# Embedding: rounded turns from one multiplication into 32-bit integers, in place of adding and subtracting a large constant

## The chip, the cores and the metric

The kernel runs on one core of a Trainium2 chip. The metric is the device time of one execution in microseconds (us); lower is better. The program is a small vision model: a sine and cosine embedding of four images, one attention layer with relative positions, an MLP, a second attention layer and a mixture of experts. The change touches only the embedding, the first some 295 us of the span.

## What the embedding must compute

For every coordinate and each of six frequencies (powers of two), the reference takes sin and cos of 2 pi times coordinate times frequency, and multiplies the 6912 features of a token with a weight matrix:

```python
xb = 2.0 * jnp.pi * xyz[..., None] * freq_bands
feat = jnp.concatenate([jnp.sin(xb), jnp.cos(xb)], axis=-1)
feat = feat.reshape(b, n, -1)
return jnp.einsum('bnf,of->bno', feat, W)
```

The kernel reduces the angle first: the turn is x f minus the nearest whole number, which lies within half a turn, and sin and cos are taken of 2 pi times that.

## The kernel before

`embed_phase` works through four images. The 576 coordinates of an image lie in five chunks of up to 128 partitions, x[128, 5, 512] (512 tokens along the free side). A **group** is one frequency for two chunks (1024 elements for each partition), twelve in an image (pair groups), or, for the last chunk, whose 64 coordinates are there twice, two frequencies at once (512 elements), three in an image. So an image has 15 groups, and the buffers `near`, `turn`, `feat` and `parts` are rings of three groups (`NF`). The order of each engine is written out by hand; semaphores count groups.

For each group, by engine and line:

- VectorE (DVE): `shift` (L202) writes x f + 12582912 into `near`; adding that constant (1.5 times 2 to the 23) leaves no room for a fraction in a float32. `whole` (L207) subtracts it again in place, so `near` is x f rounded to a whole number. `reduce` (L215) makes turn = x f - near in one instruction with two tensor operands. `absolute` (L221) writes the turn without its sign bit over `near`. For pair groups, `rest` (L232) subtracts from the features their first part.
- ScalarE (ACT): the sine of `turn` (L357), the cosine as a sine of a quarter turn minus the absolute turn (L359), and for pair groups `first_parts` (L370), a rounded copy of half the features.
- TensorE (PE): for the first chunk of a group `native`, 16 float32 matmuls (L427); for the second chunk `split`, 16 matmuls on the parts (L443 in the first group, else L445, and L447). All add into four PSUM banks. `split` waits for `rest` of its group.

In the first image alone the weights are split too: ACT rounds them (L364, queued behind the group's cosine), DVE subtracts (`split_weights`, L226), and PE's `split` waits for that. The first image also carries the class row: its statistics ahead of group 4 on DVE (L295, L297), square roots ahead of group 6 on ACT, its normalization ahead of group 8 on DVE (L301, L304).

In `image` (L307 to L330) DVE runs ahead in this order: `whole(g + 1)`, `reduce(g)`, `shift(g + 2)`, `absolute(g)`, `rest(g - 1)`, and in the first image `split_weights(g)`; before the loop stand two `shift` and one `whole` (L333 to L335). `shift(g + 2)` waits for the cosine of group g - 1, which reads the same third of the ring. At group 1 of each later image `take_sums` copies the sums of the image before out of PSUM (L238, L241), and the first matmul of the new image waits for it. Images 2 and 3 run in a loop, the fourth is written out. Numbers in this document count images from the first to the fourth and groups from 0 to 14.

Of the kernel before, what the change touches and what calls it, by code (L numbers as in the profile page):

```python
# [8 lines left out]
ALU = mybir.AluOpType  # L9
ACT = mybir.ActivationFunctionType  # L10
AX = mybir.AxisListType
F32 = mybir.dt.float32
F32R = mybir.dt.float32r
BF16 = mybir.dt.bfloat16
U32 = mybir.dt.uint32


B = 4
N = 512
# [25 lines left out]
EXPERTS, TOPK, HID = 8, 2, 4 * D  # L45
HC = HID // 128

MAGIC = 12582912.0
NO_SIGN = 0x7FFFFFFF
TWO_PI = 6.283185307179586  # L50
EPS = 1e-5
# [1 line left out]
GROUPS = [(c0, 2, f) for c0 in (0, 2) for f in range(BANDS)] + [(4, 1, j) for j in range(BANDS // 2)]  # L53
UNITS = [(c0 + i, f) for c0, n, f in GROUPS for i in range(n)]
NE = len(GROUPS)
# [8 lines left out]
def stand_alone(eng, passed):  # L64


    eng.sem_inc(passed, 1)


def embed_phase(nc, s):  # L70

    NF = 3
    sem = s.sem
# [1 line left out]
    raw_in = [sem(f"raw_in{g}") for g in range(NE)]  # L75
    freq_in, ident_in, cls_in, zeroed = sem("freq_in"), sem("ident_in"), sem("cls_in"), sem("zeroed")
    consts_set, edges_set = sem("consts_set"), sem("edges_set")
    shifted, rounded, turn_done, aturn_done = sem("shifted"), sem("rounded"), sem("turn_done"), sem("aturn_done")
    sin_done, cos_done, feat_free, passed = sem("sin_done"), sem("cos_done"), sem("feat_free"), sem("turns_passed")
    w_hi, w_lo, hi_done, lo_done = sem("w_hi"), sem("w_lo"), sem("hi_done"), sem("feat_lo")  # L80
    pairs = [g for g in range(NE) if GROUPS[g][1] == 2]
# [10 lines left out]
    with ExitStack() as ctx:  # L92
        sb = lambda n, sh, dt=F32: ctx.enter_context(nc.sbuf_tensor(n, sh, dt))
        x = sb("x", [128, 5, N])
# [2 lines left out]
        feat = sb("feat", [128, NF, 2, 2, N])  # L97
        w_parts = sb("w_parts", [128, NPAIR, 2, 2, D], F32R)
        parts = sb("parts", [128, NF, 2, 2, N], F32R)
        near = sb("near", [128, NF, 2, N])  # L100
        turn = sb("turn", [128, NF, 2, N])
        aturn = near
        tokens, h1_tok = sb("tokens", [128, 4, D]), sb("h1_tok", [128, 4, D])
        b2_rows, base = sb("b2_rows", [128, D]), sb("base", [128, 4, D])
        stats, mean_var = sb("stats", [128, 4, 6]), sb("mean_var", [128, 4, 2])
# [2 lines left out]
        freq = sb("freq", [128, NU])  # L108
# [78 lines left out]
        def _(dve):  # L187
# [1 line left out]
            dve.memset(eps[:, 0:1], EPS).then_inc(consts_set, 1)  # L189
            dve.memset(eps[:, 1:2], EPS * EPS).then_inc(consts_set, 1)  # L190

            def shift(b, g, first):
                c0, n, f = GROUPS[g]
                u, r = first_unit[g], g % NF
                if f == 0:
                    for c in range(c0, c0 + n):
                        dve.wait_ge(x_in[c], b * 16 + 16)
                if g >= NF or not first:
                    dve.wait_ge(cos_done, b * NE + g - NF + 1)
                if not first:  # L200
                    stand_alone(dve, passed)
                dve.tensor_scalar(near[:, r, 0:n, :], x[:, c0:c0 + n, :], freq[:, u:u + 1], MAGIC, ALU.mult, ALU.add).then_inc(shifted, 1)  # L202

            def whole(b, g):
                n, r = GROUPS[g][1], g % NF
                dve.wait_ge(shifted, b * NE + g + 1)
                dve.tensor_scalar(near[:, r, 0:n, :], near[:, r, 0:n, :], MAGIC, None, ALU.subtract).then_inc(rounded, 1)  # L207

            def reduce(b, g, first):
                c0, n, f = GROUPS[g]  # L210
                u, r = first_unit[g], g % NF
                dve.wait_ge(rounded, b * NE + g + 1)
                if g >= NF or not first:
                    dve.wait_ge(sin_done, b * NE + g - NF + 1)
                dve.scalar_tensor_tensor(out=turn[:, r, 0:n, :], in0=x[:, c0:c0 + n, :], scalar=freq[:, u:u + 1], in1=near[:, r, 0:n, :],  # L215
                                         op0=ALU.mult, op1=ALU.subtract).then_inc(turn_done, 1)

            def absolute(b, g):
                n, r = GROUPS[g][1], g % NF
                dve.wait_ge(turn_done, b * NE + g + 1)  # L220
                dve.tensor_scalar(aturn[:, r, 0:n, :].bitcast(U32), turn[:, r, 0:n, :].bitcast(U32), NO_SIGN, None,  # L221
                                  ALU.bitwise_and).then_inc(aturn_done, 1)

            def split_weights(g):
                dve.wait_ge(w_hi, g + 1)
                dve.tensor_tensor(w_parts[:, g, :, 1, :], raw[:, g], w_parts[:, g, :, 0, :].bitcast(F32),  # L226
                                  ALU.subtract).then_inc(w_lo, 1)

            def rest(b, g):
                r = g % NF  # L230
                dve.wait_ge(hi_done, b * NPAIR + g + 1)
                dve.tensor_tensor(parts[:, r, 1], feat[:, r, :, 1, :], parts[:, r, 0].bitcast(F32), ALU.subtract).then_inc(lo_done, 1)  # L232

            def take_sums(i):
                dve.wait_ge(base_set, i + 1)
                for m in range(4):
                    dve.wait_ge(sums_done, i * 4 + m + 1)
                    dve.tensor_copy(tokens[:, m, :], sums[m][:, 0:D]).then_inc(stated, 1)  # L238
                for m in range(4):
                    dve.wait_ge(stated, i * 8 + m + 1)  # L240
                    dve.tensor_tensor(tokens[:, m, :], tokens[:, m, :], sums[m][:, D:2 * D], ALU.add).then_inc(tokens_done, 1)  # L241
                for m in range(4):
                    dve.wait_ge(tokens_done, i * 4 + m + 1)
                    dve.bn_stats(stats[:, m, :], tokens[:, m, :]).then_inc(stated, 1)
                dve.wait_ge(rooted, i + 1)
                dve.wait_ge(stated, i * 8 + 8)
                stand_alone(dve, passed)
                for m in range(4):
                    dve.bn_aggr(mean_var[:, m, :], stats[:, m, :]).then_inc(aggregated, 1)
# [30 lines left out]
            def normalize(i):  # L280
                dve.wait_ge(rooted, i + 2)
                dve.reciprocal(inv[:, :, :], roots[:, :, :]).then_inc(inverted, 1)
                dve.wait_ge(inverted, i + 1)
                stand_alone(dve, passed)
                for m in range(4):
                    dve.tensor_scalar(s.y[:, bass.ds(i, 1), m, :].rearrange("p b n -> p (b n)"), tokens[:, m, :], mean_var[:, m, 0:1], inv[:, 0, m:m + 1],
                                      ALU.subtract, ALU.mult).then_inc(y_ready, 1)
                dve.wait_ge(h1_flipped, i * 2 + 2)
                for m in range(4):
                    dve.tensor_scalar(h1_tok[:, m, :], tokens[:, m, :], mean_var[:, m, 0:1], inv[:, 1, m:m + 1],  # L290
                                      ALU.subtract, ALU.mult).then_inc(h1_ready, 1)

            def cls_statistics():
                dve.wait_ge(cls_in, 32)
                dve.bn_stats(cls_stats[:, :], cls_row[:, 0, :]).then_inc(cls_stated, 1)  # L295
                dve.wait_ge(cls_stated, 1)
                dve.bn_aggr(cls_mean_var[:, :], cls_stats[:, :]).then_inc(cls_stated, 1)  # L297

            def cls_norm():
                dve.wait_ge(cls_rooted, 1)  # L300
                dve.reciprocal(cls_inv[:, :], cls_roots[:, :]).then_inc(cls_rooted, 1)  # L301
                dve.wait_ge(cls_rooted, 2)
                for k, row in enumerate((s.y_cls[:, :], cls_row[:, 1, :])):
                    dve.tensor_scalar(row, cls_row[:, 0, :], cls_mean_var[:, 0:1], cls_inv[:, k:k + 1],  # L304
                                      ALU.subtract, ALU.mult).then_inc(cls_rows, 1)

            def image(b, first=False, more=True):  # L307
                for g in range(NE):
                    if first and g == 4:
                        cls_statistics()  # L310
                    if first and g == 8:
                        cls_norm()
                    if g + 1 < NE:
                        whole(b, g + 1)
                    elif more:
                        whole(b + 1, 0)
                    reduce(b, g, first)
                    if g + 2 < NE:
                        shift(b, g + 2, first)
                    elif more:  # L320
                        shift(b + 1, g + 2 - NE, False)
                    absolute(b, g)
                    if g - 1 in pairs:
                        rest(b, g - 1)
                    if first and g in pairs:
                        split_weights(g)
                    if not first and g == 1:
                        take_sums(b - 1)
                    if not first and g == 4:
                        normalize(b - 1)  # L330

            dve.wait_ge(freq_in, 16)
            shift(0, 0, True)  # L333
            shift(0, 1, True)
            whole(0, 0)  # L335
            image(0, first=True)
            dve.wait_ge(cls_flipped, 1)
            dve.tensor_copy(cls_col[:, :], cls_flip[0:DC, 0:2]).then_inc(cls_cols_set, 1)
# [1528 lines left out]
def experts_phase(nc, s):  # L1867
# [28 lines left out]
    with ExitStack() as ctx:  # L1896
# [4 lines left out]
        score, top = sb("score", [1, B, EXPERTS]), sb("top", [1, B, 8])  # L1901
        index = sb("index", [1, B * 8], U32)
        both_exps, total, inv = sb("both_exps", [1, 2, B, 8]), sb("total", [1, B]), sb("inv", [1, B])
# [583 lines left out]
```

## Time and profile before

| what | value |
|---|---|
| three runs, median (lowest to highest) | 997.32 us (993.51 to 999.99) |
| span of the profiled execution | 993.9 us |
| TensorE matmuls, busy in the span | 890.0 us (90%) |
| TensorE weight loads | 787.2 us (79%) |
| VectorE | 728.3 us (73%) |
| ScalarE | 647.6 us (65%) |
| GpSimd | 141.7 us (14%) |

PE stands for TensorE's matmuls, PEld for its weight loads, which overlap them; DVE is VectorE, ACT is ScalarE. Busy shares are means over stages with different limits, so a stage has to be looked at by itself: what each engine did in it, where it idled, and which instruction ended the idling. In a time line each row gives the start and the length in us, the engine, the line, the operation and its tiles; the end of a row may overlap the start of the next by some hundredths, so what an instruction costs its engine is the distance between two starts. Idle time stands at a row's end in brackets with what ended it.

### The profile page before, as it was taken

To read this page: it belongs to the slowest core of one execution; us is meant where nothing else is said; L and a number is where in the kernel's file an instruction comes from. 1 tells how busy PE (TensorE), PEld (TensorE's weight loads), DVE (VectorE), ACT (ScalarE), POOL (GpSimd) and SP (SyncE) were. 2 spreads that over 40 slices of the span, in tenths; PEclk is the share of its full clock that TensorE was granted. 3 is DMA by queue.
4 is the path that set the end of the run, shared out by engine and by line. 5 is a ranking of instruction groups with operands and counts; after the bars stand their busy time and mean duration, and the time that the engine had idled before them with its cause. 6 is when DMAs were issued, how large, how long until landed. Compare 5 with 4: busy or idle time off the path is not lost. (4 is left out here: it accounts for less than half of the span.)

```text
span 993.9 us, 20032 instructions
## 1 busy us (share of the span) xinstructions
PE 890.0 (90%) x6459; PEld 787.2 (79%) x6459; DVE 728.3 (73%) x1703; ACT 647.6 (65%) x1218; POOL 141.7 (14%) x204
## 2 busy tenths in 40 slices
PE   5999999999998789898989898899699996799996
PEld 5899999999986577667766776676498875799995
DVE  6899979979944597569757965787567335687785
ACT  4765857757824597669767975897554321876862
POOL 1000000000001043304430432144400000000000
PEclk9999999999997899999999999999889999699998
DMA  8003110169931597259715961697210021442201
GB/s 274 22 23 99 38 33 0 37 105 139 138 58 41 154 278 233 59 155 285 221 51 172 291 202 47 196 273 214 66 43 1 14 84 32 134 147 91 78 2 63
DMA packets 83801, 114.11 MB, mean 115 GB/s; under 512 B 12271, under 2 KB 44476, under 8 KB 83724
## 3 DMA queue, kind: packets, MB, share of 16 engines
q1 hardware_dynamic: 82636, 112.39, 41.8%
q8 instruction: 37, 0.61, 0.3%
q10 hardware_dynamic: 1088, 0.79, 0.2%
q14 instruction: 40, 0.33, 0.1%
HBM read 62.31 MB, written 47.67 MB: 111 GB/s over the span
## 5 line engine op out<-in xcount | busy, mean ns | idle before, releaser
L427 PE MATMUL psum<-w,feat 128*128 128x192 f32 x912 | 160.3, 331 | 13.9 <-ACT feat L357 10.1
L427 PEld LDWEIGHTS psum<-w,feat 128*128 128x128 f32 x912 | 149.1, 192 | 14.7 <-issue 11.4
L656 POOL TENSOR_SCALAR a_scores<-a_scores,a_inv 112x514 f32<-112x514 f32 (+1 forms) x160 | 112.6, 705 | 269.5 <-DVE a_inv L1028 269.2
L1013 DVE CUSTOM_DVE_ANT_0 a_scores<-psum,a_bias 112x514 f32<-112x514 f32 (+1 forms) x160 | 110.0, 688 | 46.2 <-PE psum L732 37.7
L885 ACT ACTIVATE a_scores<-a_scores,a_least 112x514 f32<-112x514 f32 (+1 forms) x160 | 116.7, 729 | 9.8 <-DVE a_least L1013 9.2
L745 PE MATMUL psum<-ident,a_scores 112*112 112x112 f32 (+1 forms) x800 | 99.4, 255 | 19.8 <-DVE a_probsT L1023 14.5
L445 PE MATMUL psum<-w_parts,parts 128*128 128x384 f32 x368 | 112.8, 371 | 3.3 <-DVE parts L232 2.8
L357 ACT ACTIVATE feat<-turn 128x1024 f32<-128x1024 f32 (+1 forms) x60 | 58.4, 974 | 85.2 <-DVE turn L215 53.9
L745 PEld LDWEIGHTS psum<-ident,a_scores 112*112 112x112 f32 (+1 forms) x800 | 74.7, 133 | 41.7 <-issue 19.7
L732 PE MATMUL psum<-a_kh,a_q 128*112 128x258 f32 (+1 forms) x320 | 99.1, 331 | 1.0 <-DVE a_least L1013 1.0
L447 PE MATMUL psum<-w_parts,parts 128*128 128x192 f32 x384 | 96.5, 251 | 0.0
L683 PE MATMUL psum<-h1T,place 96*128 (+3 forms) x320 | 87.2, 407 | 4.7 <-DVE a_q L977 2.2
L880 ACT COPY a_probsT<-psum 112x336 f32<-112x336 f32 (+1 forms) x160 | 66.4, 415 | 28.6 <-PE psum L745 24.5
L732 PE MATMUL psum<-a_kl,a_q 128*112 128x258 f32 (+1 forms) x320 | 83.7, 282 | 0.0
L714 PE MATMUL psum<-a_table,a_qpos 96*112 96x257 bf16 (+1 forms) x320 | 65.4, 286 | 12.9 <-DVE a_pos L1003 6.3
L872 ACT COPY a_pos<-psum 112x514 f32<-112x514 f32 (+1 forms) x92 | 54.0, 587 | 31.8 <-PE psum L714 29.5
L445 PEld LDWEIGHTS psum<-w_parts,parts 128*128 128x128 f32 x368 | 69.2, 188 | 5.5 <-issue 5.3
L447 PEld LDWEIGHTS psum<-w_parts,parts 128*128 128x128 f32 x384 | 73.3, 191 | 0.0
L683 PEld LDWEIGHTS psum<-h1T,place 96*128 96x128 f32 (+1 forms) x320 | 59.6, 202 | 15.9 <-DVE a_q L977 2.9
L215 DVE SCALAR_TENSOR_TENSOR turn<-x,freq,near 128x1024 f32<-128x1024 f32 (+1 forms) x60 | 70.2, 1170 | 0.0
L359 ACT ACTIVATE feat<-near,half_pi 128x1024 f32<-128x1024 f32 (+1 forms) x60 | 63.5, 1058 | 6.8 <-DVE near L221 6.5
L1023 DVE COPY a_probsT<-psum 112x224 f32<-112x224 f32 (+1 forms) x160 | 58.8, 367 | 7.9 <-PE psum L745 7.2
(298 smaller groups left out, 1819.0 us busy)
## 6 DMA issues: line engine op xcount, KB each, us to landing
shear<-a_pos SPq DMA_DIRECT2D x128, 224.9 KB, 3.9
a_bias<-shear SPq DMA_DIRECT2D x128, 224.4 KB, 3.9
shear<-zero SPq DMA_DIRECT2D x20, 448.9 KB, 18.1
e_fc<-in_e_fc_dram SPq DMA_DIRECT2D x16, 384.0 KB, 3.9
x<-in_xT_dram SPq DMA_DIRECT2D x20, 256.0 KB, 3.0
e_proj<-in_e_proj_dram SPq DMA_DIRECT2D x8, 576.0 KB, 5.6
shear<-a_pos SPq DMA_DIRECT2D x32, 130.5 KB
a_bias<-shear SPq DMA_DIRECT2D x32, 130.3 KB
```

Source lines behind the costliest of these rows:

```text
L215: dve.scalar_tensor_tensor(out=turn[:, r, 0:n, :], in0=x[:, c0:c0 + n, :], scalar=freq[:, u:u + 1], in1=near[:, r, 0:n, :], op0=ALU.mult, ...
L427: mm = pe.matmul(sums[m][:, 0:D], feat[:, r, j, 0, 128 * m:128 * m + 128], w[:, k, :], start=begins, stop=ends)
L445: pe.matmul(sums[m][:, 0:2 * D], f(0), w_parts[:, g, j, :, :].rearrange("p a n -> p (a n)"), start=False, stop=False)
L447: mm = pe.matmul(sums[m][:, 0:D], f(1), w_parts[:, g, j, 0, :], start=False, stop=False)
L656: pool.tensor_scalar(row, row, inv[0:TILES[g % NT][1], g % TT:g % TT + 1], 1.0, ALU.mult, ALU.mult).then_inc(weighed, 1)
L683: mm = pe.matmul(out[:, 0:HALF], wt[0:rows, c, 128 * p:128 * p + 128], x, start=c == 0, stop=c == 1)
L714: mm = pe.matmul(pairs[2][w][0:r, 0:HALF], qpos[:, h, i0:i0 + r], table[:, w * HALF:w * HALF + HALF], start=True, stop=True)
L732: mm = pe.matmul(pairs[score_pair(g)][w][0:r, 0:HALF + 1], q[:, h, i0:i0 + r], k[:, h, w * HALF:w * HALF + HALF + 1], start=k is kh, stop= ...
L745: mm = pe.transpose(pairs[3][jb // 3][0:TILE, TILE * (jb % 3):TILE * (jb % 3) + r], scores[0:r, g % TT, TILE * jb:TILE * jb + TILE], s.ide ...
L880: act.copy(probsT[:, slot(g // NT), 0:3, i0:i0 + r], src).then_inc(put_a, 1)
L885: act.activation(scores[0:r, g % TT, 0:PADL], scores[0:r, g % TT, 0:PADL], ACT.Exp, bias=least[0:r, g % TT:g % TT + 1], scale=-1.0, accum_ ...
L1013: dve.tensor_tensor_reduce(halves(scores[0:r, g % TT, 0:PADL]), psum2(score_pair(g), r), halves(bias[0:r, g % MR, :]), -1.0 / 8, BIG, ALU. ...
```

## The change

`shift` and `whole` become one instruction: `near` is declared as 32-bit integer, and x f, with no constant added, is written into it, so that the conversion on the way out does the rounding. `reduce` then subtracts an integer tensor. Where the absolute turn is stored, the same memory is read as float32, as before. The semaphore `shifted` and the constant go.

```diff
@@ -97,9 +97,9 @@
         feat = sb("feat", [128, NF, 2, 2, N])
         w_parts = sb("w_parts", [128, NPAIR, 2, 2, D], F32R)
         parts = sb("parts", [128, NF, 2, 2, N], F32R)
-        near = sb("near", [128, NF, 2, N])
+        near = sb("near", [128, NF, 2, N], I32)
         turn = sb("turn", [128, NF, 2, N])
-        aturn = near
+        aturn = near[:, :, :, :].bitcast(F32)
         tokens, h1_tok = sb("tokens", [128, 4, D]), sb("h1_tok", [128, 4, D])
         b2_rows, base = sb("b2_rows", [128, D]), sb("base", [128, 4, D])
         stats, mean_var = sb("stats", [128, 4, 6]), sb("mean_var", [128, 4, 2])
@@ -189,7 +189,7 @@
             dve.memset(eps[:, 0:1], EPS).then_inc(consts_set, 1)
             dve.memset(eps[:, 1:2], EPS * EPS).then_inc(consts_set, 1)
 
-            def shift(b, g, first):
+            def whole(b, g, first):
                 c0, n, f = GROUPS[g]
                 u, r = first_unit[g], g % NF
                 if f == 0:
@@ -199,12 +199,7 @@
                     dve.wait_ge(cos_done, b * NE + g - NF + 1)
                 if not first:
                     stand_alone(dve, passed)
-                dve.tensor_scalar(near[:, r, 0:n, :], x[:, c0:c0 + n, :], freq[:, u:u + 1], MAGIC, ALU.mult, ALU.add).then_inc(shifted, 1)
-
-            def whole(b, g):
-                n, r = GROUPS[g][1], g % NF
-                dve.wait_ge(shifted, b * NE + g + 1)
-                dve.tensor_scalar(near[:, r, 0:n, :], near[:, r, 0:n, :], MAGIC, None, ALU.subtract).then_inc(rounded, 1)
+                dve.tensor_scalar(near[:, r, 0:n, :], x[:, c0:c0 + n, :], freq[:, u:u + 1], None, ALU.mult).then_inc(rounded, 1)
 
             def reduce(b, g, first):
                 c0, n, f = GROUPS[g]
@@ -310,15 +305,11 @@
                         cls_statistics()
                     if first and g == 8:
                         cls_norm()
-                    if g + 1 < NE:
-                        whole(b, g + 1)
-                    elif more:
-                        whole(b + 1, 0)
                     reduce(b, g, first)
                     if g + 2 < NE:
-                        shift(b, g + 2, first)
+                        whole(b, g + 2, first)
                     elif more:
-                        shift(b + 1, g + 2 - NE, False)
+                        whole(b + 1, g + 2 - NE, False)
                     absolute(b, g)
                     if g - 1 in pairs:
                         rest(b, g - 1)
@@ -330,9 +321,8 @@
                         normalize(b - 1)
 
             dve.wait_ge(freq_in, 16)
-            shift(0, 0, True)
-            shift(0, 1, True)
-            whole(0, 0)
+            whole(0, 0, True)
+            whole(0, 1, True)
             image(0, first=True)
             dve.wait_ge(cls_flipped, 1)
             dve.tensor_copy(cls_col[:, :], cls_flip[0:DC, 0:2]).then_inc(cls_cols_set, 1)
```

On VectorE, the first rows of the embedding's first image show it. Before (`near` is the rounded product, `turn` the reduced angle, `w_parts` the split weights, `parts` the split features):

```order
L202 TENSOR_SCALAR near<-x,freq 128x1024
L207 TENSOR_SCALAR near<-near 128x1024 [waits shifted] x2
L215 SCALAR_TENSOR_TENSOR turn<-x,freq,near 128x1024 [waits rounded]
L202 TENSOR_SCALAR near<-x,freq 128x1024
L221 TENSOR_SCALAR near<-turn 128x1024 [waits turn_done]
L226 TENSOR_TENSOR w_parts<-place,w_parts 128x2x192 [waits w_hi]
L207 TENSOR_SCALAR near<-near 128x1024 [waits shifted]
L215 SCALAR_TENSOR_TENSOR turn<-x,freq,near 128x1024 [waits rounded]
```

The same place of the changed kernel, where L215 has become L210, L221 L216 and L226 L221:

```order
L202 TENSOR_SCALAR near<-x,freq 128x1024
L210 SCALAR_TENSOR_TENSOR turn<-x,freq,near 128x1024 [waits rounded]
L202 TENSOR_SCALAR near<-x,freq 128x1024
L216 TENSOR_SCALAR near<-turn 128x1024 [waits turn_done]
L221 TENSOR_TENSOR w_parts<-place,w_parts 128x2x192 [waits w_hi]
L210 SCALAR_TENSOR_TENSOR turn<-x,freq,near 128x1024 [waits rounded]
```

Two L207 stood ahead of the first reduction and a third ahead of the second; none does now, and nothing else has changed place.

Further on in the first image, the pass over group 3 before (L207 belongs to group 4, L202 to group 5, L232 to group 2):

```order
L207 TENSOR_SCALAR near<-near 128x1024 [waits shifted]
L215 SCALAR_TENSOR_TENSOR turn<-x,freq,near 128x1024 [waits sin_done,rounded]
L202 TENSOR_SCALAR near<-x,freq 128x1024 [waits cos_done]
L221 TENSOR_SCALAR near<-turn 128x1024 [waits turn_done]
L232 TENSOR_TENSOR parts<-feat,parts 128x1024 [waits hi_done]
L226 TENSOR_TENSOR w_parts<-place,w_parts 128x2x192 [waits w_hi]
```

And now (L232 has become L227):

```order
L210 SCALAR_TENSOR_TENSOR turn<-x,freq,near 128x1024 [waits sin_done,rounded]
L202 TENSOR_SCALAR near<-x,freq 128x1024 [waits cos_done]
L216 TENSOR_SCALAR near<-turn 128x1024 [waits turn_done]
L227 TENSOR_TENSOR parts<-feat,parts 128x1024 [waits hi_done]
L221 TENSOR_TENSOR w_parts<-place,w_parts 128x2x192 [waits w_hi]
```

The reduction now follows straight on the weights' subtraction of the group before; the rows of ScalarE, TensorE, GpSimd and the DMA queue stand as they stood.

## Rows read from the trace of the kernel before

**Rows 1.** Stretch (start:end, length), busy us (instructions) of PE, PEld, DVE, ACT, POOL; PEclk, DMA share, GB/s
```profile
10.14:88.22 78.08, 71.61 (x438) 68.71 (x438) 69.49 (x104) 54.77 (x63) 0.00 (x0) 1.00 0.33 104
88.22:156.86 68.64, 67.68 (x445) 67.35 (x445) 62.47 (x98) 46.24 (x48) 1.81 (x1) 1.00 0.08 26
156.86:225.58 68.72, 67.67 (x444) 67.41 (x445) 62.52 (x98) 46.54 (x49) 1.82 (x1) 1.00 0.29 56
225.58:294.93 69.35, 67.86 (x444) 67.37 (x444) 55.35 (x92) 41.71 (x44) 1.81 (x1) 1.00 0.93 115
```

**Rows 2.** Waits of PE, 10 to 83 us: who waits, for whom, us, times, longest
```profile
PE psum L445 <- DVE parts L232: 2.8, 3, 1.4
```

**Rows 3.** Waits of PE, 98 to 290 us, later images
```profile
PE psum L427 <- DVE tokens L241: 2.0, 2, 1.0
```

**Rows 4.** Time line of PE, second image, starts of groups 2 and 3
```profile
98.26 2.79 PE L427 MATMUL psum<-w,feat 128*128 128x192 f32 x16
...
103.15 2.79 PE L427 MATMUL psum<-w,feat 128*128 128x192 f32 x16
```

**Rows 5.** Time line of PE, first image and the next two turns
```profile
16.69 0.44 PE L443 MATMUL psum<-w_parts,parts 128*128 128x192 f32 x2 [1.48 <-DVE parts L232]
...
19.22 1.00 PE L427 MATMUL psum<-w,feat 128*128 128x192 f32 x5
...
49.88 0.41 PE L445 MATMUL psum<-w_parts,parts 128*128 128x384 f32 x1 [1.44 <-DVE parts L232]
...
55.87 0.41 PE L445 MATMUL psum<-w_parts,parts 128*128 128x384 f32 x1 [0.88 <-DVE parts L232]
...
78.53 7.99 PE L427 MATMUL psum<-w,feat 128*128 128x192 f32 x48
88.22 1.08 PE L427 MATMUL psum<-w,feat 128*128 128x192 f32 x5 [1.71 <-DVE tokens L241]
...
156.86 2.87 PE L427 MATMUL psum<-w,feat 128*128 128x192 f32 x16 [0.95 <-DVE tokens L241]
```

**Rows 6.** Time line of DVE, one turn of the loop, first image
```profile
18.11 1.28 DVE L215 SCALAR_TENSOR_TENSOR turn<-x,freq,near 128x1024 f32<-128x1024 f32 x1
19.30 0.75 DVE L202 TENSOR_SCALAR near<-x,freq 128x1024 f32<-128x1024 f32 x1
19.96 0.69 DVE L221 TENSOR_SCALAR near<-turn 128x1024 uint32<-128x1024 uint32 x1
...
22.27 0.56 DVE L226 TENSOR_TENSOR w_parts<-place,w_parts 128x384 fp32r<-128x384 f32 x1 [0.48 <-ACT w_parts L364]
22.74 0.69 DVE L207 TENSOR_SCALAR near<-near 128x1024 f32<-128x1024 f32 x1
23.34 1.28 DVE L215 SCALAR_TENSOR_TENSOR turn<-x,freq,near 128x1024 f32<-128x1024 f32 x1
```

**Rows 7.** Time line of ACT in the same turn of the loop
```profile
20.68 1.15 ACT L359 ACTIVATE feat<-near,half_pi 128x1024 f32<-128x1024 f32 x1 [0.21 <-DVE near L221]
21.74 0.49 ACT L364 CAST w_parts<-place 128x384 fp32r<-128x384 f32 x1
```

**Rows 8.** Time line of DVE at the start
```profile
6.43 1.28 DVE L207 TENSOR_SCALAR near<-near 128x1024 f32<-128x1024 f32 x2
7.63 1.27 DVE L215 SCALAR_TENSOR_TENSOR turn<-x,freq,near 128x1024 f32<-128x1024 f32 x1
```

**Rows 9.** Time line of DVE, reductions of groups 6, 7 and 8, first image
```profile
39.50 1.28 DVE L215 SCALAR_TENSOR_TENSOR turn<-x,freq,near 128x1024 f32<-128x1024 f32 x1
...
46.06 1.28 DVE L215 SCALAR_TENSOR_TENSOR turn<-x,freq,near 128x1024 f32<-128x1024 f32 x1
...
52.06 1.27 DVE L215 SCALAR_TENSOR_TENSOR turn<-x,freq,near 128x1024 f32<-128x1024 f32 x1
```

**Rows 10.** Casts of one tensor on DVE: ns min/median/max, first and last start us, forms
```profile
L994 DVE CAST a_kl<-a_kl x32: 407/420/558, 314.8 to 644.5; 64x514 fp32r<-64x514 f32 x32
...
L945 DVE CAST a_table<-place x1: 705/705/705, 302.6 to 302.6; 96x514 bf16<-96x514 f32 x1
```

More of the change, by code:

```diff
@@ L15 @@
 U32 = mybir.dt.uint32
+I32 = mybir.dt.int32
 B = 4
@@ L46 @@
 HC = HID // 128
-MAGIC = 12582912.0
 NO_SIGN = 0x7FFFFFFF
@@ L77, in embed_phase @@
     consts_set, edges_set = sem("consts_set"), sem("edges_set")
-    shifted, rounded, turn_done, aturn_done = sem("shifted"), sem("rounded"), sem("turn_done"), sem("aturn_done")
+    rounded, turn_done, aturn_done = sem("rounded"), sem("turn_done"), sem("aturn_done")
     sin_done, cos_done, feat_free, passed = sem("sin_done"), sem("cos_done"), sem("feat_free"), sem("turns_passed")
```

## The prediction

> **What bounds the kernel now.** I first read the busy time of each engine in four stretches, one for each image of the embedding [rows 1]. A stretch runs from the first matmul of one image to the first of the next. TensorE (PE) is busy for 67.7 of 68.6 us in the second image and 67.7 of 68.7 in the third: there VectorE (DVE, 62.5 us busy) waits for PE, not the other way round. The first image is another case: it takes 78.1 us, and PE does no more in it (438 matmuls recorded against 444 or 445). So about 9.5 us of the 993.9 us span are lost in the first image, and the later ones lose next to nothing. Everything after the embedding is untouched by the change and moves with its end.
>
> Next, who held PE up. In the first image the list of waits puts PE's longest repeated wait on the subtraction at L232, the second operand of the split matmuls [rows 2]; in the later images only short waits remain, mainly 2.0 us in two pieces for the sums to be read out of PSUM at the turn of an image [rows 3]. The time line gives PE's own pace for a group of two chunks: 98.26 to 103.15 us, 4.89 us [rows 4]. In the first image the reductions (L215) come at 18.11 and 23.34, 5.23 us apart [rows 6].
>
> Why 5.23? It is a loop over two engines. From the start of L215 (18.11) DVE goes to L202 of the group two ahead (19.30), then the absolute value L221 (19.96); ScalarE (ACT) then takes the cosine (20.68 [rows 7]), and behind it the weight cast L364 (21.74); that releases L226 on DVE (22.27), and then follow L207 (22.74) and the next L215 (23.34) [rows 6, 7]. Only the first image has L364 and L226, so only there is this loop closed. It is slower than PE's 4.89.
>
> **The change part by part.** *Removed: L207, 60 times.* One of 1024 elements is recorded at 0.69 us, but the next instruction starts 0.60 us after it (22.74 to 23.34 [rows 6]); 0.60 us is what the path loses. 48 of the 60 lie in pair groups. The 45 of the later images stand beside PE work that sets the pace [rows 1], so I cost them at nothing; without that cover they would be worth up to 36 x 0.60 + 9 x 0.34 (estimated as 0.60 scaled by the shorter tile), some 25 us. The same cover hides the sums at the turn of an image: 0.95 us of PE idling there [rows 5] runs from PE's last matmul through the copies to the first sum, with no L207 in it.
>
> *The start.* Two L207 stand ahead of the first L215: 6.43 to 7.63, 1.20 us [rows 8]. A third stands ahead of the second L215, 0.60 us more. PE's first split matmul waits for L232 of group 0, which is queued behind that second L215, so it moves from 16.69 [rows 5] by 1.80 to 14.89, and PE starts group 1 at 19.22 - 1.80 = 17.42.
>
> *The rest of the first image.* The loop falls to 5.23 - 0.60 = 4.63, below PE's 4.89, so PE becomes late next and sets the pace. From 17.42, eleven pair groups take 11 x 4.89 = 53.8, the three short groups 7.99 us as now, and the turn 0.95 as in the third image [rows 5]: the second image starts at 80.2 in place of 88.22, a gain of 8.0 us including the 1.8.
>
> *What is given back.* Two steps of the loop are longer: L215 goes from 39.50 to 46.06 (6.56) where ACT takes the class row's square root, and on to 52.06 (6.00) where DVE normalizes that row [rows 9]. PE idles 1.44 and 0.88 us for them [rows 5]. The first will stay near 6.55, because ACT is what is busy in it; the second falls to 5.40. The loop's lead over PE is what pays: about 0.7 us at group 1 (L232's result ready at 14.89 + 4.63 = 19.5, wanted 2.8 us after 17.42) and 0.26 more with each group, less half a us for the class row's statistics, so 1.2 us. The two steps overrun PE's pace by 1.66 and 0.51, so about 1.0 us of idling is left; 2.3 would be left if nothing were won. I take 1.2. Sum: 8.0 - 1.2 = 6.8 us.
>
> *Changed: L202 writes integers and drops its addition.* Before, it takes 0.75 us and the next starts after 0.66 [rows 6]. No VectorE arithmetic that turns float32 into a 32-bit integer is in this trace. The low bound is that of L207 without a column operand, 0.69; the high bound is the price of one element at a time, which for 1024 elements is the 1.28 of L215, which reads two tensors. The nearest casts disagree: 514 elements to the split type (L994) in a median of 420 ns, 514 to bfloat16 (L945) in 705 ns [rows 10]. L945 halves the element and ran once; L994 keeps four bytes as the change does, so I take 0.75. In the loop L202 stands ahead of L221; at 1.28 it would add 0.53, so the loop would be 5.16.
>
> The Trainium skill ("Vector Engine (DVE) Microarchitecture Reference", 5.1 Performance modes) asks of the two-port mode one source, both ends in SBUF and matching even shapes, and names no element type; by it the integer write keeps its speed and the sum is 6.8. L945 meets those conditions and does not agree at 705 ns; going by that row the sum would be under 1.
>
> *Changed: L215 subtracts an integer tensor.* No row has mixed operands. A gain is excluded, since its other tensor is still read as float32; it is 1.28 now, and I take 1.28. The high bound is twice one element at a time, 0.53 x 2 = 1.06 more.
>
> *Moved.* Rounding group g + 2 now stands where its L202 stood, with the same wait for the cosine of group g - 1; no DMA, wait or other engine's work is moved, and one semaphore goes.
>
> **The rivals.** *(B) Integers are written one element at a time.* For it: L945; against it: L994. The loop is 5.16 against 5.23: eleven steps of 0.07 are 0.8, and at the start two writes 0.53 longer eat 1.06 of the 1.20. Gain about 0.9: 996.4.
>
> *(C) PE's own work sets the first image too.* For it: PE's weight loads are busy 68.7 of 78.1 us, close to DVE's 69.5 [rows 1]; a PE bound there would leave only the earlier start, 1.8 us: 995.5. Against it: the matmuls are those of the other images, which finish in 68.6, and the idling before L445 ends on DVE [rows 2]. The Trainium skill ("Perfetto Trace Analysis", Identifying the Most-Contended Engine) ranks engines by occupancy, TensorE by its weight loads; on the whole span that names TensorE, by which a cut on DVE brings little. By that rule this rival is the likely one; the idle rows of the first image speak against it.
>
> *(D) Slower: mixed types cost L215 a second pass.* From 1.28 to 2.34, the loop is 4.63 + 1.06 = 5.69, 0.46 over today, 5 us in the first image. DVE would also have about 67 us of work in each later image (62.5 less 9.5 for fifteen L207, plus 14.3), so close to PE's 68.7 that up to 2 us at each turn could be added: +5 to +11, say 1005. It decides from L215 above 1.28 + 0.60 = 1.88 us. Nothing in the trace speaks for it, except that no such row exists.
>
> *(E) More.* DVE's new lead removes all idling in the first image and the two turns after it: 8.0 + 2.0 = 10: 987.3.
>
> **How the numbers follow.** The profiled execution spans 993.9 us; the runs shown are 993.5 to 1000.0 with a median of 997.3, so this profile is at their low end. I take the gain of 6.8 off its span (987.1) and off the median: 990.5. Chances: forecast 0.66, B 0.15, C 0.10, D 0.04, E 0.05. The forecast's own range is 986.5 to 994.5 (the unsure idling of about 1 us each way, and the runs' scatter of 3 us). The range, 985.5 to 997.5, takes in B, C and E and leaves out D and the tails. One per cent is about what a measurement of this kernel can tell from no change, and is 10 us here: faster by more needs a gain that only E has, or the forecast with three us of scatter to its favour: 0.15. Slower by more needs D at its upper end: 0.03. The rest, 0.82, lies within 1%.
>
> **What would show it.** Right: L202 still near 0.75 us and L215 near 1.28; L215 of the first image about 4.6 apart until ACT or DVE runs ahead and PE's ring of three buffers holds them; PE's first split matmul near 14.9; the first image some 71 us long in place of 78.1; the next three unchanged at 68.6 to 69.4; the three pieces in which L445 waits for L232 in the first image [rows 2] down to two or fewer. Wrong: L202 near 1.28 (B), L215 near 2.3 (D), a first image of 76 us with quick DVE instructions (C), or later images that become shorter (then DVE did hold PE up where the trace shows no idling).

## The result and the profile after

| | before | after |
|---|---|---|
| median of 20 runs each (lowest to highest) | 998.09 us (992.60 to 1273.90) | 992.24 us (985.24 to 998.49) |
| ratio of the times (95% interval) | 1 | 0.9932 (0.9910 to 0.9954) |
| span of the profiled execution | 993.9 us | 990.8 us |
| first image, first matmul to first matmul | 78.08 us | 72.69 us |
| second, third, fourth image | 68.64, 68.72, 69.35 us | 68.62, 68.99, 69.60 us |
| VectorE busy in the span | 728.3 us | 696.6 us |

One of the 20 runs before took 1273.9 us, and the ratio, which goes by the other runs, leaves it out; the median of the other 19 is 997.32. The ratio is worth 6.8 us of 998.1 (interval 4.6 to 9.0); the quotient of the two medians without that run would be 0.9949, that of the means 0.9938, both inside the interval. The gain is 0.7%, inside the 1% that I called "the same", but the interval stays clear of 1.

The four stretches of the embedding, against [rows 1] (stretch and its length, then busy us and instructions of PE, PEld, DVE, ACT, POOL, the granted clock, DMA share, GB/s):

```profile
8.97:81.66 72.69, 70.26 (x439) 68.99 (x439) 60.96 (x88) 54.37 (x63) 0.00 (x0) 1.00 0.35 116
81.66:150.28 68.62, 67.67 (x444) 67.38 (x444) 54.50 (x83) 46.04 (x49) 1.81 (x1) 1.00 0.08 26
150.28:219.27 68.99, 67.94 (x445) 67.67 (x445) 54.53 (x83) 46.16 (x49) 1.81 (x1) 1.00 0.30 58
219.27:288.87 69.60, 68.12 (x444) 67.62 (x444) 49.18 (x80) 41.28 (x44) 1.81 (x1) 1.00 0.80 112
```

Each of the four stretches holds 6 to 8.5 us less VectorE work. Only the first is shorter, by 5.39 us, and it begins 1.17 us earlier (8.97 against 10.14), so the second image starts 6.56 us earlier.

One turn of the loop in the time line of VectorE, against [rows 6]:

```profile
15.72 1.28 DVE L210 SCALAR_TENSOR_TENSOR turn<-x,freq,near 128x1024 f32<-128x1024 f32 x1
16.92 0.75 DVE L202 TENSOR_SCALAR near<-x,freq 128x1024 int32<-128x1024 f32 x1
17.58 0.69 DVE L216 TENSOR_SCALAR near<-turn 128x1024 uint32<-128x1024 uint32 x1
...
19.89 0.56 DVE L221 TENSOR_TENSOR w_parts<-place,w_parts 128x384 fp32r<-128x384 f32 x1 [0.48 <-ACT w_parts L354]
20.36 1.28 DVE L210 SCALAR_TENSOR_TENSOR turn<-x,freq,near 128x1024 f32<-128x1024 f32 x1
```

Reductions are 4.64 us apart in place of 5.23. The integer write takes 0.75 us as the float write did, and the reduction with an integer operand 1.28 as before. Everything up to the weights' subtraction keeps its distance; what is gone is the 0.60 us behind it.

TensorE's idle time in the first image and at its end, from its time line, against [rows 5]:

```profile
8.97 5.23 PE L417 MATMUL psum<-w,feat 128*128 128x192 f32 x16 [8.97 <-ACT feat L347]
14.91 0.44 PE L433 MATMUL psum<-w_parts,parts 128*128 128x192 f32 x2 [0.71 <-DVE parts L227]
...
45.12 0.41 PE L435 MATMUL psum<-w_parts,parts 128*128 128x384 f32 x1 [0.49 <-DVE parts L227]
...
50.51 0.41 PE L435 MATMUL psum<-w_parts,parts 128*128 128x384 f32 x1 [0.28 <-DVE parts L227]
...
81.66 1.57 PE L417 MATMUL psum<-w,feat 128*128 128x192 f32 x8 [0.95 <-DVE tokens L236]
```

Of the waits for the second operand (L232, now L227), that of group 0 is half as long as before (0.71 against 1.48 us), and those at groups 6 and 7 are a third as long (0.49 and 0.28 against 1.44 and 0.88). The turn to the second image costs 0.95 us, as the later ones do (0.95 and 1.05).

**One profile against one profile misleads here.** The embedding ends 6.1 us earlier (288.87 against 294.93), but the span is only 3.1 us shorter. From there to the first cast of the attention phase 6.35 us pass in place of 7.64. The change touches no instruction there, and experiments 3 and 4, which remove none, show 6.4 us too; the cause of these 1.3 us is not shown. The two stretches behind, from the first cast of the attention phase to its last matmul and from there to the end, after and then before:

```profile
295.22:701.70 406.48, 368.37 (x2864) 286.32 (x2864) 285.43 (x844) 303.08 (x709) 122.14 (x173) 0.97 0.58 175
701.70:990.76 289.06, 250.60 (x1786) 232.66 (x1785) 183.30 (x447) 150.62 (x302) 8.53 (x20) 0.90 0.21 65
```

```profile
302.57:710.10 407.53, 364.88 (x2864) 283.68 (x2864) 285.20 (x844) 303.39 (x709) 121.79 (x173) 0.98 0.58 174
710.10:993.86 283.76, 244.97 (x1786) 227.87 (x1785) 183.30 (x447) 150.78 (x302) 8.51 (x20) 0.93 0.22 66
```

The last stretch, which the change does not touch and which has the same instructions, took 5.3 us more at a granted clock (TensorE's, as a share of full speed) of 0.90 in place of 0.93; so 6.1 + 1.3 + 1.0 - 5.3 gives the 3.1. That clock varies from run to run of one and the same kernel: of 17 runs of the kernel before on one chip, the three with a mean granted clock of 0.966 took 994 to 995 us, the two with 0.954 took 1006 and 1008. So where six us are at stake, the stretch is compared in the profile and the whole over many runs.

### The profile page after: what moved, and what is told of

Read it like the earlier page. It is cut to its first block and busy times, and to the rows that moved or that the text cites. A ratio compares the mean times of both kernels' runs of the same rounds, so it can differ in the third digit from the quotient of the medians.

```text
span 990.8 us, 19970 instructions
## 1 busy us (share of the span) xinstructions
PE 896.9 (91%) x6459; PEld 794.4 (80%) x6459; DVE 696.6 (70%) x1643; ACT 645.6 (65%) x1218; POOL 142.0 (14%) x204
## 5 line engine op out<-in xcount | busy, mean ns | idle before, releaser
L210 DVE SCALAR_TENSOR_TENSOR turn<-x,freq,near 128x1024 f32<-128x1024 f32 (+1 forms) x60 | 70.9, 1182 | 0.3 <-DVE h1T L331 0.3
L202 DVE TENSOR_SCALAR near<-x,freq 128x1024 int32<-128x1024 f32 (+1 forms) x60 | 41.6, 695 | 40.3 <-ACT feat L349 32.5
```

## The experiments

Theory: the gain comes from the first image alone, where VectorE and ScalarE form a loop (reduction, next rounding, absolute value, cosine, weight cast, weights' subtraction, and before the change the subtraction of the constant) that was slower than TensorE. Rival: VectorE has less to do, wherever that is.

**1. Integers in the first image alone.** `INT_FIRST` is True; `first` tells the first image.

```diff
+        near_int = near[:, :, :, :].bitcast(I32)
...
+                if first == INT_FIRST:
+                    dve.tensor_scalar(near_int[:, r, 0:n, :], x[:, c0:c0 + n, :], freq[:, u:u + 1], None, ALU.mult).then_inc(rounded, 1)
+                else:
+                    dve.tensor_scalar(near[:, r, 0:n, :], x[:, c0:c0 + n, :], freq[:, u:u + 1], MAGIC, ALU.mult, ALU.add).then_inc(shifted, 1)
```

> The first image writes integers as in the change; the three later images keep adding and subtracting the constant. If the gain comes from the first image's loop alone: the first image (first matmul to the first of the second image) takes 72.7 us as in the change against 78.1 before, the later ones 68.6 to 69.4 as before, and the time falls by 6 to 7 us, ratio about 0.993. Rival, less VectorE work is worth the same wherever it is taken away: 15 of the 60 removed instructions, a quarter of the gain, 1.5 us, ratio 0.998 to 0.999.

Measured: 993.09 us against 999.17 of the kernel before on the same chip, ratio 0.9934 (0.9903 to 0.9965). The four stretches:

```profile
9.02:81.71 72.69, 70.72 (x438) 69.26 (x439) 62.70 (x91) 54.39 (x63) 0.00 (x0) 1.00 0.36 116
81.71:150.60 68.89, 67.94 (x444) 67.64 (x444) 62.49 (x98) 46.47 (x49) 1.81 (x1) 1.00 0.08 26
150.60:219.33 68.73, 67.68 (x444) 67.41 (x445) 62.52 (x98) 46.54 (x49) 1.81 (x1) 1.00 0.30 55
219.33:288.67 69.34, 67.86 (x444) 67.37 (x444) 55.37 (x92) 41.71 (x44) 1.81 (x1) 1.00 0.94 116
```

The first stretch is that of the change, 72.69 us; a quarter of the removed instructions bring all of the gain. The rival's 0.998 to 0.999 lies outside the interval.

**2. Integers in the later images alone.** The same kernel with `INT_FIRST = False`.

> The reverse: the first image adds and subtracts the constant, the three later images write integers. If the gain comes from the first image alone: first image 78.1 us as before, later ones 68.6 to 69.6, no gain, ratio 0.999 to 1.001 although VectorE does 45 of the 60 removed instructions less. Rival, VectorE work counts everywhere: three quarters of the gain, 4.5 to 5 us, ratio 0.995.

Measured: 998.03 us against 999.17, ratio 0.9985 (0.9955 to 1.0015). The rival's 4.5 to 5 us (0.9955 to 0.995) lie at the interval's edge and just outside it, so the time alone hardly decides. The profile does:

```profile
10.38:87.73 77.35, 71.96 (x438) 68.83 (x438) 67.88 (x101) 54.42 (x63) 0.00 (x0) 1.00 0.34 106
87.73:156.37 68.64, 67.68 (x445) 67.39 (x445) 54.57 (x83) 46.06 (x49) 1.82 (x1) 1.00 0.08 26
156.37:225.09 68.72, 67.67 (x444) 67.40 (x445) 54.54 (x83) 46.15 (x49) 1.81 (x1) 1.00 0.30 58
225.09:294.44 69.35, 67.86 (x444) 67.37 (x444) 49.20 (x80) 41.28 (x44) 1.81 (x1) 1.00 0.91 113
```

VectorE does 8 us less in the second and third image, 54.5 in place of 62.5, and they last as long as before to 0.01 us. The first is 0.7 us shorter than the 78.1 I had expected: the turn to the second image idles 0.95 us in place of 1.71 [rows 5], since VectorE handles the second image's first groups ahead of the sums and now comes to these earlier. Experiment 1 idles 0.96 there too, so either part of the change brings this 0.75 us, the one piece of the gain that doesn't need the loop.

**3. The order alone.** Every instruction of the kernel before is kept; in the first image the subtraction of the constant moves into a gap.

```diff
-                    if g + 1 < NE:
+                    if not first and g + 1 < NE:
                         whole(b, g + 1)
...
+                    if first:
+                        whole(b, g + 1) if g + 1 < NE else whole(b + 1, 0)
                     if first and g in pairs:
                         split_weights(g)
```

> The kernel before with every instruction kept; in the first image alone the subtraction of the constant stands ahead of the weights' subtraction, in the 0.48 us in which VectorE idles for ScalarE's weight cast, in place of behind it. If the loop over the two engines is what sets the first image: its step falls from 5.23 to about 4.75 us, below TensorE's 4.89, the first image takes about 73 us, and the time falls by 5.5 to 6 us, ratio 0.994, with as much VectorE work as before. Rival, the amount of VectorE work is what counts: the step stays at 5.2, first image 78 us, ratio 1.000.

Measured: 994.85 us against 999.17, ratio 0.9951 (0.9921 to 0.9982). The loop in the time line of VectorE:

```profile
16.68 1.27 DVE L215 SCALAR_TENSOR_TENSOR turn<-x,freq,near 128x1024 f32<-128x1024 f32 x1
...
19.14 1.22 DVE L232 TENSOR_TENSOR parts<-feat,parts 128x1024 fp32r<-128x1024 f32 x1
20.27 0.68 DVE L207 TENSOR_SCALAR near<-near 128x1024 f32<-128x1024 f32 x1
20.87 0.55 DVE L226 TENSOR_TENSOR w_parts<-place,w_parts 128x384 fp32r<-128x384 f32 x1
21.34 1.28 DVE L215 SCALAR_TENSOR_TENSOR turn<-x,freq,near 128x1024 f32<-128x1024 f32 x1
```

A step takes 4.66 us with L207 in it, and there is no idle time ahead of L226 any more: L207 fills the 0.48 us in which VectorE waited for the cast. The first image takes 72.86 us (9.88 to 82.74) with VectorE as busy as before, 69.5 us. The second image starts 5.5 us earlier without one instruction less.

**4. The cast earlier.** Every instruction of the kernel before is kept; ScalarE rounds the weights ahead of the sine.

```diff
-                group(0, g, True)
                 if g in pairs:
                     split_weights(g)
+                group(0, g, True)
+                if g in pairs:
                     first_parts(0, g)
```

> The kernel before with every instruction kept; ScalarE alone is changed: in the first image it casts a group's weights ahead of the sine of that group, where it idles, in place of behind its cosine. If the loop through that cast sets the first image: the loop is opened, VectorE runs its six instructions back to back (1.19 + 0.66 + 0.61 + 1.14 + 0.47 + 0.60 = 4.67 us a step), TensorE at 4.89 becomes the bound, the second reduction starts 1.7 us earlier, the second image starts at about 81.3 in place of 88.2 and the time falls by about 6.5 us, ratio 0.9935. Rival, the subtraction of the constant is too much work for VectorE in the first image whatever stands around it: step 5.2, ratio 1.000.

Measured: 993.22 us against 999.17, ratio 0.9946 (0.9916 to 0.9977). All of TensorE's waits between 11 and 82 us:

```profile
PE psum L428 <- DVE tokens L241: 1.0, 1, 1.0
```

The second image starts at 81.35 us (expected 81.3), and the first takes 71.07. The step is 4.66 us, from one reduction (15.97) to the next (20.63). With the loop opened, VectorE's six instructions run back to back and TensorE is never held up before the turn, the two long steps included. At group 6, where the class row's square root is taken, VectorE's step is 4.66 too (35.09 to 39.75): ScalarE's cast (36.97) stands ahead of its switch back to the sine's table (37.48) and of the group's sine and cosine. The later one, where VectorE normalizes the class row, still takes 5.44, without holding TensorE up. The subtraction of the constant was not too much work; it stood in the wrong place.

**5. Both: the change with the early cast.**

> The changed kernel with the weight cast ahead of the sine as well. If the loop through that cast is the only thing that still holds TensorE up in the first image: VectorE's step there is 4.07 us of work, the second reduction starts at about 9.5 in place of 11.1, the split matmuls of group 0 follow on the native ones without idling (14.2), the idling at groups 6 and 7 (0.49 and 0.28 us) goes, the second image starts at about 80 in place of 81.7, and the time is 1.5 to 2 us below that of the change: ratio to the kernel before 0.991 to 0.992. Rival, ScalarE becomes the bound (3.8 us of work a group plus the table switch for the class row): the idling at group 6 stays and the ratio is 0.993.

Measured: 990.32 us against 997.04, ratio 0.9917 (0.9884 to 0.9950). VectorE's step:

```profile
17.41 1.27 DVE L210 SCALAR_TENSOR_TENSOR turn<-x,freq,near 128x1024 f32<-128x1024 f32 x1
18.60 0.74 DVE L202 TENSOR_SCALAR near<-x,freq 128x1024 int32<-128x1024 f32 x1
19.27 0.68 DVE L216 TENSOR_SCALAR near<-turn 128x1024 uint32<-128x1024 uint32 x1
19.87 1.21 DVE L227 TENSOR_TENSOR parts<-feat,parts 128x1024 fp32r<-128x1024 f32 x1
21.00 0.55 DVE L221 TENSOR_TENSOR w_parts<-place,w_parts 128x384 fp32r<-128x384 f32 x1
21.47 0.34 DVE L290 BATCH_NORM_STATS2 cls_stats<-cls_row 1x6 f32<-1x192 f32 x1
```

It is 4.06 us (17.41 to 21.47, where the next reduction would start but for the class row). The second image starts at 78.69, 3.0 us earlier than in the change and better than the 80 expected: group 0's split matmuls follow at 13.13, since the slow native ones (below) ended at 13.4 and not at 14.2. TensorE idles nowhere in the first image before the turn. Over the whole the gain on the change is about 1.5 us by the ratios, whose intervals overlap; the profile of the first image carries this verdict, not the total.

**6 to 8. TensorE not starting from a standstill.** In the change the first 16 matmuls take 5.23 us, nearly twice what 16 later ones take (2.79 [rows 4]), at a granted clock that is shown as 1.00. In the kernels that begin with them they take 4.33 to 5.46 us. So the kernel of experiment 5, the early cast included, with idle matmuls (on zeros, their result unread) ahead of them:

```diff
+            pe.wait_ge(edges_set, 1)
+            for _ in range(18):
+                pe.matmul(s.bank[7][:, 0:171], zero[:, 0:128], zero[:, :], start=True, stop=True)
```

> The same as e5_after_early_cast with 18 further matmuls on a zeroed tile at the very start, whose result nothing reads, so that TensorE does not begin with its features. In the change the first 16 matmuls take 5.23 us, at 320 ns each, where 16 later ones take 2.79, at 163. If that is because TensorE had stood still: the 16 take about 2.8 us, group 0's split matmuls start at about 13.3 when their operand is ready, the second image starts at about 79, 1 us earlier: ratio 0.990 to 0.991. Rival, the first 16 are slow for another reason (operands that arrive late): they stay at 5.2 us and the time is that of e5_after_early_cast.

Measured: 998.21 us against 997.04, ratio 1.0001 (0.9969 to 1.0034): both theories missed. The start of TensorE's time line:

```profile
1.04 7.66 PE L406 MATMUL psum<-zero 112*128 112x171 f32 x36 [1.04 <-POOL zero L173]
9.88 2.84 PE L421 MATMUL psum<-w,feat 128*128 128x192 f32 x16 [1.19 <-ACT feat L347]
```

The theory was right on the 16: they take 2.84 us, so what slowed them was that TensorE had stood still. The gain was wrong even there, since split matmuls then wait for VectorE (13.45), and the second image starts at 78.95, no earlier than in experiment 5. And some 8 us were lost behind the embedding, which ends at 285.90 here and at 285.65 there. TensorE's list of waits in the whole span (releaser "issue": nothing that the profile shows) has, first of all, a row that neither the kernel before nor the change has:

```profile
PE psum L672 <- issue: 4.8, 2, 2.5
```

L672 is the first matmul of a new image in the attention phase. Its first three images run in a loop and the fourth is written out. The two pauses stand at the two jumps back of that loop (415.63 and 516.62 us); the change to the fourth image, which needs no jump, has none (616.31). So I changed the number of idle matmuls, first to 16:

> As e6_warm with 16 in place of 18 idle matmuls. In e6_warm the embedding ended as early as in e5_after_early_cast, but TensorE paused 2.2 and 2.5 us at two turns of the attention phase's loop over images (415.6 and 516.6 us), put down to nothing that the profile shows, and the granted clock fell to 0.5 behind the second. If the pauses come from where the loop's instructions lie in TensorE's stream, which the added ones shift: another count shifts them elsewhere, the pauses go or change, and without them the time is that of e5_after_early_cast or 1 us less, ratio 0.990 to 0.992. Rival, they come from TensorE being busy from the start: they stay at 2.2 and 2.5 us, ratio 1.000.

Measured: 997.34 us against 1000.34, ratio 0.9980 (0.9946 to 1.0013). The second turn of the attention loop:

```profile
514.52 1.57 PE L763 MATMUL psum<-place,a_on 128*128 128x192 f32 x8 [0.49 <-ACT a_on L885]
518.64 2.85 PE L672 MATMUL psum<-place,a_h 96*112 96x256 f32 x12 [2.55 <-issue]
```

The pauses stay, 2.4 and 2.5 us, and again the change to the fourth image has none. Then to 12:

> As e8_warm16 with 12 idle matmuls. By the place of the instructions: the pauses at the loop's turns are there or not by the count alone, not growing with it. By the busy start: they stay or shrink in proportion to the count, to 1.5 us.

Measured: 989.13 us against 1000.34 (six runs), ratio 0.9893 (0.9836 to 0.9951). The same turn:

```profile
509.94 1.57 PE L763 MATMUL psum<-place,a_on 128*128 128x192 f32 x8 [0.49 <-ACT a_on L885]
511.34 2.77 PE L672 MATMUL psum<-place,a_h 96*112 96x256 f32 x12
```

No pause is left, at either jump. The 12 still keep TensorE busy from 1.04 to 6.4 us and the first 16 feature matmuls still take 2.84, so a busy start alone does not cause the pauses: they are there or not by how many instructions are added ahead of the loop. With more of them the busy start is longer as well (to 8.3 and 8.7 us); that this is not what matters is argued, from some 400 us of other work in between and from the jumps. The Trainium skill ("Runtime: NRT & Kernel Launch", Instruction fetch mechanics) says that an engine's instructions are fetched in blocks in order, and that a taken branch to a block which is not at hand waits for it. The runs agree in that the pauses stand at the loop's jumps back and come and go with the number of instructions ahead, 2.2 to 2.5 us each; that a fetch is what takes them is argued, not shown. The two pauses are 5 us. Right behind the second, experiment 6 has one more stretch at half clock (granted 0.50, the lower of the two levels, for 3.4 us from 517 us on): the first 12 matmuls of that image take 4.53 us, against 2.77 where the fourth image begins. That is 1.8 us more; where the rest went is not settled. The kernel with 12 has the lowest median here, but its first image ends no earlier than in experiment 5 (78.61 against 78.69), so its lead over that one is not shown to be more than scatter.

**9. The cast that had gone the other way.** My high bound for the integer write leaned on L945 [rows 10]. The changed kernel with that cast made three times:

```diff
+            dve.tensor_copy(table[:, :], s.raw_table).then_inc(again, 1)
+            dve.wait_ge(again, 1)
+            dve.tensor_copy(table[:, :], s.raw_table).then_inc(again, 1)
+            dve.wait_ge(again, 2)
             dve.tensor_copy(table[:, :], s.raw_table).then_inc(table_set, 1)
```

> The changed kernel with the cast of the position table to bfloat16 (96 partitions, 514 elements, 705 ns in the kernel before) made three times in a row, the second and third after GpSimd's fills beside it have ended. If a cast that halves the element goes one element at a time: all three take about 700 ns. If the fills beside it slowed it: the second and third take 400 to 480 ns. Device time some 1 us above the change.

The three in the time line of VectorE:

```profile
295.92 0.70 DVE L936 CAST a_table<-place 96x514 bf16<-96x514 f32 x1 [1.26 <-PEq L92]
296.66 0.43 DVE L938 CAST a_table<-place 96x514 bf16<-96x514 f32 x1
297.12 0.43 DVE L940 CAST a_table<-place 96x514 bf16<-96x514 f32 x1
```

And what GpSimd did then:

```profile
295.88 0.11 POOL L629 MEMSET a_bias<- 112x5 f32 x1 [4.27 <-POOLq L92]
295.92 0.26 POOL L630 MEMSET a_scores<- 112x184 f32 x1
...
296.19 0.16 POOL L633 MEMSET a_probsT<- 112x25 f32 x1
```

The cast to bfloat16 takes 0.43 us once GpSimd's fills beside it have ended, so its 0.70 is not the price of halving the element, and the row on which rival B rested did not speak for it at all. That the fills took the 0.27 us fits the rows; that the first of the three also is VectorE's first instruction of its phase is not separated from it. (One run: 992.16 us.)

## Why the prediction was right, point by point

- **Forecast 990.5 us, measured 992.24; forecast gain 6.8 us, measured ratio worth 6.8.** The base was right: the 997.3 of three runs is also the median of the 19 runs above. That the gain agrees to the tenth is luck, with an interval from 4.6 to 9.0 and medians 5.1 us apart (997.32 and 992.24); so is how near the time came, since medians of the kernel before went from 997.0 to 1000.3 over the four sets of runs in this study. The mechanism is held up by the first image, where the second image was forecast 6.8 us earlier and came 6.56 earlier.
- **The prices.** Integer write 0.75 us (a median of 746 ns over 60), the reduction with an integer operand 1.28 (1277 ns): both as taken. B and D fell with that. (For D the prediction counted 9.5 us for the fifteen L207 of a later image, by their recorded lengths; VectorE's busy time there fell by 8.0.)
- **The start.** Forecast 14.89 for the first split matmul and 17.42 for group 1; measured 14.91 and 17.44.
- **The loop.** Forecast 4.63, measured 4.63 to 4.64 in regular steps; the two long steps 6.55 and 5.41, forecast 6.55 and 5.40. Experiments 3 and 4 show that the loop, not the amount of work, is the cause: 4.66 with every instruction kept.
- **What is given back.** Forecast 1.2 us at groups 6 and 7. The idle time there is 0.77 us, but TensorE's two steps take 5.61 and 5.39 us (41.84 to 47.45 to 52.84) in place of 4.88, so 1.24 us are lost: here a wait cost more than the idle time that is listed. The prediction's own working gave 1.0 of idling and took 1.2 without a reason, so that this term is met so closely is luck in part. The second image was forecast at 80.2 plus 1.2, 81.4, and starts at 81.66: I left out the class row's transposes on TensorE, with which the step from group 10 to 11 takes 5.16 in place of 4.89 (62.60 to 67.76). The "some 71 us" among the signs leaves the 1.2 out; with it the sum gives 72.4 for the first image, and 72.69 was measured.
- **The later images at no gain.** Experiment 2: 8 us of VectorE work less, 0.00 to 0.01 us shorter. The third and fourth image of the change are 0.27 and 0.25 longer than before. I had not foreseen that. In the third image TensorE's steps are 4.92 us in place of 4.88 over the first seven groups, with no idle time, and as before from there on; why is open. It is not the integers, since experiment 2 has 68.72 and 69.35 with them, and the second image of experiment 1 has 68.89 without.
- **C**, that TensorE's own work sets the first image, fell: 72.69 us in place of the 76 it gives, and 69.6 in experiment 5 shows what TensorE needs. The Trainium skill's ranking of engines by occupancy ("Perfetto Trace Analysis", Identifying the Most-Contended Engine), on which it leaned, names TensorE when it is taken over the whole span, by its weight loads (79% before, against 73% for VectorE); the idle rows of the one stretch found this gain.
- **E**, that all idling goes, did not come true for the change (0.71 us at group 0, 0.77 at groups 6 and 7, and the turns remain); experiment 5 comes nearest.

## What to carry to other kernels

Where an engine is idle a little in every step of a loop that crosses two engines, an instruction on the path between them costs its full length, and the same instruction in the gap costs next to nothing (a step of 4.66 us with it, 4.64 without): look for the order first. Experiments 3 and 4 removed nothing, and their second image starts at 82.74 and 81.35 us, against 81.66 with the change and 88.22 before. Read the bottleneck from the stretch, not the span: three quarters of the work taken off VectorE here bought next to nothing, one quarter bought all that the time can tell. And when a change of a few instructions moves a stretch that it does not touch, look for pauses that nothing in the profile explains at the jumps of loops, and for another granted clock, before believing a cause.

## What the runs showed of the hardware

- VectorE writes float32 products as 32-bit integers at the speed of float32 (746 against 745 ns for 1024 elements), and reads an integer tensor as the second operand at that of float32 (1277 against 1275).
- A VectorE cast of 514 elements from float32 to bfloat16 took 705 ns beside GpSimd fills of 0.1 to 0.3 us, 430 behind them.
- TensorE's first 16 feature matmuls took 5.23 us in the change after standing still (4.33 in experiment 5, 5.46 in experiment 4) and 2.84 after 12, 16 or 18 idle ones, all shown at a granted clock of 1.00.
- Matmuls added ahead on TensorE put 2.2 to 2.5 us into both jumps back of a loop 400 us later, or not, by how many they are (12 no, 16 and 18 yes).
